# Cross-attention and ternary FFN on one core: the high half of the FFN input in fp16, hidden-layer units in pairs

## What is computed

```
h = bitlinear(x, w_fc) + gate * (x @ v.T @ fast_b.T @ u.T)     # 512 -> 2048, plus a low-rank term
r = maximum(h, 0)
y = bitlinear(r * r, w_proj)                                   # 2048 -> 512
x = x + xattn(layernorm(x), ctx);  x = x + y(layernorm(x))
# bitlinear: weights are -1, 0 or +1 times one scale for each output row
```

## Time and profile before

| | |
|---|---|
| median of 3 runs | 780.21 us (779.91 to 780.46) |
| the profiled execution | 779.99 us, its span 778.2 us |
| TensorE matmul busy | 766.5 us (98%), 3767 matmuls |
| TensorE weight load busy | 637.6 us (82%), beside the matmuls |
| VectorE / ScalarE / GpSimd busy | 547.6 / 368.6 / 107.4 us |
| granted TensorE clock | 1.0 |

### The profile page before, as it was taken

The page is one execution under the profiler, slowest core; times in us unless marked ns, Lnnn a source line. Parts: engine busy times, 40 slices in busy tenths (PEclk is TensorE's granted clock), DMA queues, the critical chain, the costliest instruction groups (busy, mean ns, idle before and its releaser), DMA issues.

```text
span 778.2 us, 10596 instructions
## 1 busy us (share of the span) xinstructions
PE 766.5 (98%) x3767; PEld 637.6 (82%) x3767; DVE 547.6 (70%) x1118; ACT 368.6 (47%) x690; POOL 107.4 (14%) x125
## 2 busy tenths in 40 slices
PE   7999999999999999999999999999999999999997
PEld 4678788888888888888888888888888888888886
DVE  5999766778676777667766786768667686656434
ACT  5998744354434535354434545254542644233332
POOL 3101300100211030110312020210202002100001
PEclk9999999999999999999999999999999999999999
DMA  8743431163115322063214422063212430040101
GB/s 315 248 150 109 63 88 41 21 96 87 56 40 84 58 72 85 13 97 69 81 42 65 65 75 96 1 99 70 90 41 41 75 88 1 1 54 9 47 0 55
DMA packets 180125, 56.20 MB, mean 72 GB/s; under 512 B 167620, under 2 KB 167894, under 8 KB 180072
## 3 DMA queue, kind: packets, MB, share of 16 engines
q1 hardware_dynamic: 149940, 50.79, 26.8%
q10 hardware_dynamic: 30132, 4.73, 3.8%
HBM read 26.92 MB, written 8.39 MB: 45 GB/s over the span
## 4 chain that ended last, share of the span: by engine, by line
PE 97%; DVE 1%; ACT 1%; issue 0%; DMA 0%; DVEq 0%; ACTq 0%
PE H L1357 30%; PE O L1338 29%; PE G L1220 26%; PE H L1363 4%; PE H L1220 1%; PE H L1197 1%; PE H L1204 1%; PE O L1412 1%; PE G L1304 1%; PE O L1378 1%; PE H L1185 1%; PE G L1248 0%; DMA Wq_s<-in_L_xattn_Wq_dram 0%; DVE x2a L1057 0%; PE O L1395 0%
## 5 line engine op out<-in xcount | busy, mean ns | idle before, releaser
L1338 PE MATMUL O<-projT,qbuf 128*128 128x512 f32 x992 | 242.1, 390 | 0.0
L1338 PEld LDWEIGHTS O<-projT,qbuf 128*128 128x128 f32 x992 | 185.0, 188 | 38.2
L779 ACT ACTIVATE rbuf<-H,scf 128x512 f32<-128x512 f32 x128 | 87.5, 684 | 124.9 <-DVE qbuf L1116 75.7
L1357 PE MATMUL H<-even_group,fcT 128*128 128x512 f32 x512 | 127.5, 391 | 0.0
L1357 PE MATMUL H<-odd_group,fcT 128*128 128x512 f32 x512 | 127.3, 391 | 0.0
L1112 DVE TENSOR_TENSOR rbuf<-rbuf 128x512 f32<-128x512 f32 x128 | 91.5, 723 | 45.9 <-ACT rbuf L779 45.9
L787 ACT ACTIVATE qbuf<-rbuf 128x512 fp32r<-128x512 f32 x125 | 78.5, 628 | 89.7 <-PE O L1338 62.7
L1116 DVE TENSOR_TENSOR qbuf<-rbuf,qbuf 128x512 fp32r<-128x512 f32 x125 | 85.9, 688 | 36.5 <-ACT qbuf L787 35.8
L1357 PEld LDWEIGHTS H<-odd_group,fcT 128*128 128x128 f32 x512 | 95.3, 188 | 19.3
L1357 PEld LDWEIGHTS H<-even_group,fcT 128*128 128x128 f32 x512 | 95.1, 188 | 19.2
L1220 PE MATMUL G<-Wvo,tT 128*128 128x512 f32 x270 | 64.7, 389 | 0.0
(11 more groups left out here) (194 smaller groups left out, 989.0 us busy)
## 6 DMA issues: line engine op xcount, KB each, us to landing
xb<-in_x_dram SPq DMA_DIRECT2D x8, 1024.0 KB, 5.1
n_blocks<-n_rows SPq DMA_DIRECT2D x112, 64.0 KB, 2.3
ctxb<-in_ctx_dram SPq DMA_DIRECT2D x8, 768.0 KB, 4.3
n_blocks<-ctxb SPq DMA_DIRECT2D x112, 48.0 KB, 2.2
wring<-in_L_ffn_w_fc_dram SPq DMA_DIRECT2D x16, 256.0 KB, 6.2
wring<-in_L_ffn_w_proj_dram SPq DMA_DIRECT2D x16, 256.0 KB, 2.7
out_dram<-x2a SPq DMA_DIRECT2D x8, 512.0 KB, 2.7
x_blocks<-x_rows SPq DMA_DIRECT2D x56, 64.0 KB, 3.5
```

The source lines that it names most:

```text
L779: nc.scalar.activation(rbuf[:, j % 2, :], banks[f"H{j % 2}"][:, :], ACT.Relu, scale=scf[:, j:j + 1]).then_inc(relu_made, 1)
L1338: mm = pe.matmul(banks[f"O{t}"][:, :], qbuf[:, j % 2, h, t * P:(t + 1) * P], projT[:, j, :], start=(j == 0 and h == HI), stop=(j == NFF - ...
L1357: pe.matmul(banks[f"H{j % 2}"][:, :], fcT[:, k, j * P:(j + 1) * P], xnT[:, h, k, :], start=(k == 0 and h == HI), stop=False)
```

## The change

1. The high half of the FFN input is written in fp16 to new buffers (`hi16_of`), by the same ScalarE steps as before. The high passes of `up` take this half with the upper 16 bits of each `fcT` word, read as bf16 (`fc16`, every second 16-bit element). The low passes and the low-rank pass stay fp32r.
2. The nine passes of a unit are no longer in the order high, low, high, low. They are four of one kind, then four of the other. A unit starts with the kind that the matmul ahead of it had; after anything but a unit this is the low kind. The low-rank pass stands behind the low ones. Unit 0 of a body always starts with the high ones.
3. `L:0` needs the high half in fp32r. GpSimd makes it with copies, `x32:k`, one for each block k in a body (128x512), two of 128x2x128 for each in the prologue.
4. TensorE's lists put more units side by side: in bodies 1 to 6 `down:9` stands ahead of `up:12` and `down:11` ahead of `up:14`; in the last body, units 3 to 15 and their `down` steps go in pairs. ScalarE's and VectorE's lists follow in the last body. In bodies 1 to 6 ScalarE's `xhi3` moves ahead of `nc1+` and `hi:15`, and VectorE's `xraw3` ahead of `lo:14`; nothing else of theirs changes there.
5. In the prologue unit 0's low-rank pass is apart from its other eight: `main:0 L:0 main:1 rank:0 turn:31 rank:1 up:2` in place of `L:0 up:0 up:1 up:2 turn:31`.

```diff
     "pe": (   # bodies 1 to 6
-        ... a:3 down:7 up:10 up:11 down:8 "
-        "up:12 down:9 up:13 down:10 up:14 down:11 up:15 down:12 down:13 "
+        ... a:3 down:7 up:10 up:11 down:8 "
+        "down:9 up:12 up:13 down:10 down:11 up:14 up:15 down:12 down:13 "
     "act": (
-        ... up:14 up:15 hi:14 nc1+ nc2+ hi:15 xhi3 nc3+ "
+        ... up:14 up:15 hi:14 xhi3 nc1+ hi:15 nc2+ nc3+ "
     "dve": (
-        "sq:14 sq:15 lo:14 xraw3 xlo3 lo:15 "
+        "sq:14 sq:15 xraw3 lo:14 xlo3 lo:15 "
     "pool": (
-        "residual xs23+ a:0 a:1 a:2 a:3 cs23+ "
+        "residual xs23+ a:0 a:1 a:2 a:3 cs23+ x32:0 x32:1 x32:2 x32:3 "
     # last body, TensorE
-        "down-:14 L:0 down-:15 up:0 up:1 up:2 down:0 up:3 down:1 up:4 down:2 up:5 down:3 up:6 down:4 ...
+        "down-:14 L:0 down-:15 up:0 up:1 up:2 up:3 down:0 down:1 up:4 up:5 down:2 down:3 up:6 up:7 ...
     # prologue, TensorE
-        "... x:3 sprow B.L:0 B.up:0 B.up:1 B.up:2 turn:31 "
+        "... x:3 sprow B.main:0 B.L:0 B.main:1 B.rank:0 turn:31 B.rank:1 B.up:2 "
     # prologue, VectorE
-        "B.cs23 B.L:0 B.sq:0 round:31 B.lo:0 B.sq:1 B.lo:1 "
+        "B.cs23 round:31 B.L:0 B.sq:0 B.lo:0 B.sq:1 B.lo:1 "
+        fc16 = fcT[:, :, :].bitcast(BF16).rearrange("p k (n h) -> p k n h", h=2)[:, :, :, 1]
+        def xhi32(g, k):
+            return group_of[(g + 1) % 2 if k < 2 else g % 2][:, HI, 2 + k % 2, :]
+                    elif st[0] == "x32":
+                        k = st[1]
+                        if b < 0:
+                            pool.wait_ge(unit_act, n_act(b, ("x", k)))
+                            pool.wait_ge(rounded_made, 28)
+                            for n in (0, 1):
+                                nc.gpsimd.tensor_copy(group_of[(g + 1 + n) % 2][:, HI, 2:4, cols],
+                                                      hi16_of[0][:, 2 * n:2 * n + 2, cols]).then_inc(xhi32_made, 1)
+                        else:
+                            pool.wait_ge(xhi_made, KD * b + k + 1)
+                            nc.gpsimd.tensor_copy(xhi32(g, k), hi16_of[g % 2][:, k, :]).then_inc(xhi32_made, 1)
 # TensorE
                 elif kind == "L":
+                    highs = [(FB[:, k, :], xhi32(b, k)) for k in range(KD)]
+                    pe.wait_ge(xhi32_made, 2 * TILES + KD * b)
+            def up_half(b, j, h, start, stop):
+                for k in range(KD):
+                    ternary = (fc16 if h == HI else fcT)[:, k, j * P:(j + 1) * P]
+                    tokens = hi16_of[b % 2][:, k, :] if h == HI else group_of[b % 2][:, LO, k, :]
+                    latest["pass"] = pe.matmul(banks[f"H{j % 2}"][:, :], ternary, tokens,
+                                               start=(start and k == 0), stop=(stop and k == KD - 1))
+                latest["half"] = h
-                        for k in range(KD):
-                            for h in (HI, LO):
-                                pe.matmul(banks[f"H{j % 2}"][:, :], fcT[:, k, j * P:(j + 1) * P], xnT[:, h, k, :],
-                                          start=(k == 0 and h == HI), stop=False)
+                        halves = order_of_halves() if kind == "up" and j > 0 else (HI, LO)
+                        for h in halves:
+                            up_half(b, j, h, start=(h == halves[0]),
+                                    stop=(h == HI and h == halves[1]))
+                            if h == LO and kind == "up":
+                                low_rank(b, j, stop=(h == halves[1]))
```

More of the change, by code:

```diff
@@ L366, in mk_xattn_ffn, with under @@
         setup.close()
-        def under(name, shape):
+        def under(name, shape, dt=F32):
             with ExitStack() as below_it:
-                return sb(name, shape, F32, below_it)
+                return sb(name, shape, dt, below_it)
         raw_of = [None, under("odd_halves", [P, 2, KD, TOK])]
+        hi16_of = [None, under("odd_hi16", [P, KD, TOK], FP16)]
         odd = sb("odd_group", [P, 2, KD, TOK], F32R)
@@ L383, in mk_xattn_ffn @@
         raw_of[0] = under("even_halves", [P, 2, KD, TOK])
+        hi16_of[0] = under("even_hi16", [P, KD, TOK], FP16)
         even = sb("even_group", [P, 2, KD, TOK], F32R)
@@ L1250, in unit @@
                     xnT = group_of[b % 2]
+                    highs = [(FB[:, k, :], xhi32(b, k)) for k in range(KD)]
+                    pe.wait_ge(xhi32_made, 2 * TILES + KD * b)
                     if b == 0:
                         job_read(pe, JOBS.index(("fb", 0)))
-                        pe.wait_ge(unit_act, n_act(-1, ("x", 3)))
-                        products(bank[:, :], [(FB[:, k, :], xnT[:, HI, k, :]) for k in range(KD)], last=False)
+                        products(bank[:, :], highs, last=False)
                         pe.wait_ge(unit_dve, n_dve(-1, ("x", 3)))
@@ L1257, in unit @@
                     else:
-                        pe.wait_ge(xhi_made, KD * b)
-                        products(bank[:, :], [(FB[:, k, :], xnT[:, HI, k, :]) for k in range(KD)], last=False)
+                        products(bank[:, :], highs, last=False)
                         pe.wait_ge(xlo_made, KD * b)
@@ L1340, in down, with order_of_halves, done, low_rank @@
                 mm.then_inc(down_full, 1)
+            latest = {"pass": None, "half": LO}
+            def order_of_halves():
+                return (latest["half"], 1 - latest["half"])
+            def done(full):
+                latest["pass"].then_inc(full, 1)
+            def up_half(b, j, h, start, stop):
+                if b == 0 and j == 0:
+                    if h == HI:
+                        pe.wait_ge(unit_dve, n_dve(-1, ("x", 1)))
+                        pe.wait_ge(unit_act, n_act(-1, ("x", 3)))
+                    else:
+                        pe.wait_ge(unit_dve, n_dve(-1, ("x", 3)))
+                for k in range(KD):
[4 more added lines that the diff above has]
+                latest["half"] = h
+            def low_rank(b, j, stop):
+                if j == 0:
+                    pe.wait_ge(unit_dve, n_dve(b, ("L", 0)))
+                    if b == 0:
+                        pe.wait_ge(ut_stored, 4)
+                latest["pass"] = pe.matmul(banks[f"H{j % 2}"][:, :], uT[:, j * P:(j + 1) * P], tstack[:, :],
+                                           start=False, stop=stop)
+                latest["half"] = LO
             def steps(b, todo, odd=None):
@@ L1346, in steps @@
                         unit(b, st)
+                        latest["half"] = LO
                     elif kind == "job":
                         job(j)
[L1349 removed]
+                    elif kind in ("up", "main"):
                         if b > 0 or j >= 2:
                             pe.wait_ge(relu_made, NFF * b + j - 1)
[L1352 removed]
                         if b == 0:
                             piece_stored(pe, j)
[L1355 to L1364 removed]
+                        halves = order_of_halves() if kind == "up" and j > 0 else (HI, LO)
[4 more added lines that the diff above has]
+                                low_rank(b, j, stop=(h == halves[1]))
+                        if kind == "up":
+                            done(up_full)
+                    elif kind == "rank":
+                        low_rank(b, j, stop=True)
+                        done(up_full)
                     elif kind == "down":
                         down(b, j)
+                        latest["half"] = LO
                     elif kind == "down-":
                         down(b - 1, j)
+                        latest["half"] = LO
                     elif kind == "turn":
```

33 lines of the change are left out of this document (14 added, 19 removed), and 6 rows, old and new, of tables (BODY_ORDER, PROLOGUE).

## The result

The changed kernel takes 789.2 us (median of 4 runs, 788.79 to 791.85), against 780.34 us for the kernel before on the same chip (779.91 to 780.46): a ratio of 1.0123, 95% interval 1.0103 to 1.0142, so 8.9 us slower. The forecast was 783.9 us, with a range up to 786.0. The sign was right, the size was not. The profiled execution of the changed kernel is its slowest (791.85 us): 3.1 us of that stand ahead of the first `turn` step, while the weights are loaded and made ready, and are no part of the change: experiments 1 and 3, with the same code there, reach that step at 19.9 and 20.0 us, the kernel before at 19.6.

A forecast was written before the change was run, and what follows sets the result against it. TensorE's passes end to end were taken to bound the kernel, any wait between them paid in full. 779.99 - 3.5 (passes and changes of kind) + 6.1 (`down:9`) + 1.1 (prologue) = 783.7, adjusted to 783.9 us; range 777.5 to 786.0.

The forecast's parts named there:

- Part 1: High passes of `up`: fp16 costs 215.6 ns, 10.7 less than fp32r; 512 passes gain 5.5 us.
- Part 2: Runs of fp16 passes: 94 runs lose 1.3 us on the way in, 0.7 us (0 to 1.3) going back.
- Part 3: `down:9` ahead of `up:12`: waits 1.23 us for `lo:9` in bodies 1 to 5, 6.1 us lost; none in body 6.
- The first rival: `lo:9` comes in time for `down:9` in bodies 1 to 5: faster, 777.8 us; chance 15%.
- Part 4: Prologue: `rank:0` delays the relus of units 0 and 1 and so `up:3`; 1.1 us lost (0.8 to 1.3).
- Part 5: GpSimd's copies for `L:0`: 0.9 us each in a body, 0.48 in the prologue, all covered, cost 0.
- The rival of late copies: GpSimd's copies are late in the prologue: 785.9 us; chance 7%.
- Part 6: The rest at nothing: `xraw3` ahead of `lo:14`, the last body's pairs and tail, ScalarE's writes.
- The rival of the strided load: `fc16` loads are plain and exposed, 93 ns more for each of 94 runs: 8.7 us, 792.6 us; chance 4%.
- the fp16 passes gain nothing: Rival on the high passes: mixed accumulation sets their distance, stalls and changes of kind remain, 789.4 us; chance 4%.

The follow-up runs named there:

- experiment 1: Changed kernel with `lo:9` ahead of `sq:10` and the statistics `cs23+` in VectorE's list of bodies 1 to 6; 783.58 us, ratio 1.0040.
- experiment 3: Changed kernel with the high halves kept in fp32r, same lists and grouping, GpSimd's copies left out; 789.66 us, ratio 1.0119.
- experiment 4: Changed kernel with a unit's passes high, low, high, low again, units 0 and 1 of body 0 excepted where split; 795.71 us, ratio 1.0195.
- experiment 5: Experiment 1 with the low halves in fp16 too, low-rank pass ahead of the eight or behind them; 777.97 us, ratio 0.9969.
- experiment 2: Kernel before with only TensorE's new order in bodies 1 to 6 (`down:9` ahead of `up:12`, `down:11` ahead of `up:14`), no fp16; 787.02 us, ratio 1.0082.
- experiment 8: Changed kernel with all lists of bodies 1 to 7 as in the kernel before, GpSimd's copies added; 789.35 us, ratio 1.0117.
- experiment 9: Experiment 8 with the change's earlier places for `xhi3` and `xraw3` put back in bodies 1 to 6; 782.92 us, ratio 1.0037.
- experiment 6: Experiment 1 with TensorE's and VectorE's prologue lists of the kernel before, GpSimd's copies kept; 781.75 us, ratio 1.0020.
- experiment 10: Experiment 5 with the prologue lists of the kernel before from experiment 6; 776.01 us, ratio 0.9949.
- experiment 7: Experiment 1 with GpSimd's additions of the residual of group 1 held back until `lo:1` of body 0 is made; 782.76 us, ratio 1.0037.
- run 27: Not a follow-up run: in "behind a run 27 ns", the run is a row of fp16 passes and 27 ns the next load's lead on its pass.

## Why the prediction was right in sign and wrong in size

**Part 1, the fp16 pass: right.** 215.6 ns was worked out from 128-column passes; inside a run the distances are 215 and 216.

**Part 2, the changes of kind: the step that failed.** The way in is the 14 ns that I took. "I bound the way back by 0 and by the 14 ns of the way in, and take the middle, 7 ns" is where it broke: the way back is 4 ns in its own distance and about 40 more over the next nine passes, and a run costs 47 to 60 ns instead of 21. At that price 94 runs eat 4.4 to 5.6 us of the 5.5 gained. Experiment 3 leaves 0.5 us, and experiments 4 and 5 show that the price goes neither by the number of fp16 passes nor simply by the number of runs, but by how often a stretch of fp32r passes follows. Experiment 2 shows the ripple without any fp16 pass, so it is the price of starting a stretch of fp32r passes anew. The row was in my hands: after `turn:31` eight passes took 1.93 us instead of 1.81. I put all 120 ns down to the short matmul in front. That can hold for the first distance alone, and 25 of the 120 stand behind it: the second to sixth distances of that group are 231, 236, 228, 232 and 231 ns, the same ripple. The bound should have reached to 120 ns instead of 14, 94 x 106 ns = 10 us more at the upper end.

**Part 3, `down:9`: right** in mechanism, in place (bodies 1 to 5, not 6) and nearly in size. The start of `down:9` is late by 1.20 to 1.22 us in the five bodies (distances of 1.43 to 1.45 us instead of 0.23), where I had 1.23. What I didn't have is the restart behind the wait, 0.11 us in the next distance and 0.02 to 0.06 in the ripple: 1.33 in all (experiment 2). That bodies 1 to 5 of the changed kernel lose just 1.23 is luck: the restart and the 0.1 us that their fp16 passes gain cancel. `down:11` waits only where `lo:9` does not hold it back, in two bodies of experiment 1. The first rival, `lo:9` in time, didn't happen by itself; experiment 1 brings it about with one entry and shows its price.

**Part 4, the prologue: right in mechanism, one consequence missed.** `rank:0`, `relu:0`, `relu:1` and `up:3` are late as forecast, each by 0.2 us more than I had: `up:3` starts 1.50 us late instead of 1.25 (96.47 against 91.85, less the 3.12 of the loading). With the additions held back, `down:0` comes 1.5 us later than before (75.93 us after the first `turn`, against 74.41), above the 0.8 to 1.3 forecast. What I didn't follow is what `turn:31` releases besides TensorE's next step: GpSimd's additions. With them beside it VectorE's squares take more than twice as long, and `down:0` waits another 1.15 us. The rule that every queue behind a moved step counts was applied to TensorE and ScalarE, not to GpSimd. The trace of the kernel before already shows it, in the square of 1.16 us at 94.61.

**Part 5, the copies: right at nothing** in the changed kernel, and mostly faster than I took them: 0.63 us for 128x512 (the median of 28, from 0.61 to 1.13) and 0.40 for half of it. But the cover was thinner than my text says. Experiments 8 and 9 show that `xhi3`'s move, which I had put under the cover and not under the costs, is what hides them: without it the wait is 0.8 us a body. The rival of late copies in the prologue didn't come in the changed kernel, where `main:0` covers them; with `L:0` at its old place (experiments 6 and 10) they are late.

**Part 6: right.** Body 7 shows nothing but its fp16 passes: with the same lists and no fp16 (experiment 3) it takes 65.08 us, as before.

The rival of the strided load failed with its premise too: the load of an fp32r pass lasts 188 ns beside 512 columns and 192 beside 256, where the passes stand 120 ns apart, so it isn't bounded by 107.

The rival "the fp16 passes gain nothing" gave 789.4 us, near what was measured, but its mechanism is not the one that acts. Each pass does gain 10.7 ns. It is the changes of kind that take this back, and so experiment 5 could get below the kernel before, which under that rival it could not.

**The account.** Predicted -3.5 + 6.1 + 1.1 = +3.7. Measured: about -0.5 (experiment 3 by medians; -0.8 if 0.1 us for each of bodies 1 to 5 is added to the 0.3 outside them), +6.6 for the stall with its restart (5 x 1.33), +2.7 for the prologue. The sum is 8.5 to 8.8, beside 8.9 us by the medians. So of the 5.3 us by which the forecast is short, some 3 are the fp16 passes, 1.6 the prologue and 0.5 the restarts.

## What to carry to other kernels

Where TensorE works without a gap, the price of a special pass is not its own distance. Read the dozen distances behind it too, and give the unknown half of such a price a bound from a row, not from symmetry with the half that is known. When a consumer is moved earlier, compare the move with the slack of its producer in every body, and look first whether the producer can be exchanged with something that nobody waits for: here that was worth 5.6 us. Measure a wait from start to start: the idle time that the profile shows leaves out the overlap of two matmuls and the restart. And a step that ends a wait for two engines moves both; ask what the second one does to the engines next to it.

## What the runs showed of the hardware

- Fp32r passes of 512 columns stand 227 ns apart, but up to 240 for some five to eleven passes when a stretch of them starts anew. Behind fp16 passes this adds 20 to 47 ns in all (the changed kernel), alike behind eight and behind sixteen; behind a wait in a kernel without fp16 it adds 25 to 60 (experiment 2). With one fp32r pass between fp16 ones it does not appear in between (experiment 4).
- In a stretch of fp32r passes each weight load starts 223 ns ahead of its pass. The load of the first fp16 pass of a run starts 4 ns ahead of it, that of the first fp32r pass behind a run 27 ns, that of the first pass behind a wait 2 ns (body 7 of the changed kernel, 744 to 746 us; experiment 2, 334.69 us). The ripple follows the latter two. What makes it is open: no run here tells the weight load from the matmul.
- VectorE's additions, products and squares of 128x512 in fp32 take 0.69 us alone, and 1.49 and 1.76 us beside additions on GpSimd (0.69 and 0.68 again in experiment 7, which moves the additions away). Its 28 subtractions for `xlo` take 0.68 to 0.69 us each in experiment 3, which has no copies on GpSimd, and 1.09 to 1.11 in 14 of 28 in the changed kernel. The copies themselves took 0.61 to 1.13 us, all 28 with VectorE at work beside them; no run here shows what makes the difference.
- A wait that the profile shows as 1.02 us of idle TensorE made a body 1.33 us longer (experiment 2), with the clock granted in full (0.999): 0.16 us is the overlap of two matmuls, 0.11 the next distance, the rest the ripple.
